# Half tiles of the experts' second product: finishing and summing two at a time, early in each of 16 rounds

## The chip, the cores and the metric

One Trainium2 chip, eight cores. Each core runs the same program on its own sequence (one of eight batch entries) and none waits for another. The metric is device microseconds (us) of the slowest core. TensorE (PE in the profile) does the matmuls, ScalarE (ACT) and VectorE (DVE) move results out of the 8 PSUM banks, GpSimd (POOL) and SyncE (SP) issue DMAs; POOL also does some arithmetic.

## The reference

Per sequence of 4096 rows of width 1024: one head of attention over the whole width with residual and layer norm, then a mixture of 64 experts chosen per group of 16 rows, with residual and layer norm again.

```python
x = _layernorm(x + _L0_attn_ref(x, W_qkv, b_qkv, W_out, b_out))
# _L0_ffn_ref, on groups of 16 rows:
sel   = jnp.einsum('...btd,...btes->...besd', grouped, perm)
inner = jax.nn.relu(jnp.einsum('...besd,desf->...besf', sel, f1) + bias)
inter = jnp.einsum('...besf,esfd->...besd', inner, f2)
out   = jnp.einsum('...besd,...btes->...btd', inter, perm)
x = _layernorm(x + out)
```

The change is in the last two einsums and the layer norm behind them.

## The kernel before

The program is written out by hand, one list of instructions for each engine, in the order in which Python code calls the helpers. An engine works through its list in that order; a wait in it (on a counter of another engine or of a DMA) holds up all that stands behind it. `T`, `VE`, `C`, `GP`, `SP` are the lists of TensorE, VectorE, ScalarE, GpSimd and SyncE. Nearly all matmuls carry line 128, ScalarE's operations line 137, VectorE's lines 142 to 149.

Attention comes first, the experts' first half (`gather`, `product1`, `rectify`) goes to about 1357 us, and the second half, with which this case deals, runs from there to the end. It is a loop of 16 **rounds**, `for j in range(16)`, each of eight **steps** k (lines 982 to 1006). In a round:

- `product2(j, k)`: 8 matmuls of 64x256 into a pair of banks. From round 3 on there are only two pairs for it, banks 0 to 3, used in turn (`made_in`). Step k issues the product of step k+1, the last step that of the next round's step 0. I call them p0 to p7.
- `product2_out(j, k, q)`: copies the pair (128x1024) to `arenaA`. From round 3 on, 0 to 6 are ScalarE's, 7 is VectorE's. I call them out0 to out7. Product p(k) needs out(k-2), which clears its pair.
- `swap(j - 1)`: one VectorE transpose of 128x4096 of the round before, into `xT`; it needs all eight outs of that round.
- `combine(m)`, from round 3, four in a round: one matmul of 128x512 with the identity, which brings the residual (`hrv(m)`, from `hsp`), and four of 32x512 (the experts' values from `xT` by the choices in `permC`) into one bank of 4 to 7. This is a **half tile**: 128 rows by 512 columns of the output. The bank must have been left by the half tile of the round before. Behind each `combine` SyncE loads the residual of the half tile four further on (`load_hr`). I call the four sums of a round c0 to c3.
- `stats2(m)`, at the end of the round: VectorE's `bn_stats` on each of the four banks; where the half tile is the second half of its rows (rounds 5, 6, 9, 10, 13, 14), an aggregate behind each.
- `finish2(m)`, from round 4, the four half tiles of the round before leave their banks, by ScalarE: f0 to f3. First halves (rounds 4, 5, 8, 9, 12, 13) are copied to `YF`. Second halves (rounds 6, 7, 10, 11, 14, 15, which I call **norm rounds**) are scaled and shifted on the way to one of five small homes, from which SyncE's queue stores them to `y`; ScalarE waits there for `home_used`, the last store out of that home. For output rows 0 to 1023 (rounds 6 and 7) the home is `i % 3`, so f0 and f3 of one round share one; later it goes round all five. POOL then scales the first half (line 844) and issues its store.
- in norm rounds ScalarE also computes four reciprocal deviations (`rstd2`, two tiny operations ahead of out0, which need VectorE's four aggregates of the round before), and VectorE the shifts (`shift2`, ahead of `swap`), for which f0 waits.

Before, the places in a round were: `swap` at step 2, f0 to f3 one at a step at steps 1 to 4, each behind that step's out, and c0 to c3 at steps 2 to 5, each behind that step's product. In round 15, step 2, POOL's list also takes the loads of the residuals 52, 53, 56 and 57, which need swap(14).

Behind the loop a tail sums and norms the last half tiles (`combine_last`, `keep_last`, `pair_last`, `second_last`, `first_last`); its first instructions need residuals that POOL loads behind all of its work on rounds 14 and 15. TensorE takes the residual 58 before it goes on.

Of the kernel before, what the change touches and what calls it, by code (L numbers as in the profile page):

```python
# [49 lines left out]
def build_nc():  # L50
# [47 lines left out]
    def bank(i):  # L98
        return PS[:, i * 512:(i + 1) * 512]
# [27 lines left out]
    def mm(out, lhsT, rhs, first, last, mark=False, **kw):  # L127
        fn = lambda e, o=out, l=lhsT, r=rhs, a=first, z=last, k=kw: e.matmul(o, l, r, start=a, stop=z, **k)  # L128
        if mark:
            return T.mark(fn)  # L130
        T.do(fn)
# [4 lines left out]
    def act(out, src, func, **kw):  # L136
        return C.mark(lambda e, o=out, s=src, f=func, k=kw: e.activation(o, s, f, **k))  # L137
# [556 lines left out]
    def place(m):  # L694

        s, i = m // 8, m % 8
        return s // 2, i, s % 2, s // 2 * 8 + i

    def summed_in(m):
        return m % 4 if 56 <= m < 60 else 4 + m % 4  # L700

    def hrv(m):
        if m >= 52:
            return A[:, INP[0] + (m - 52) * 512:INP[0] + (m - 51) * 512]
        return WC[:].bitcast(BF16)[:, (m % 4) * 512:(m % 4 + 1) * 512]

    def load_hr(m, q=SP):
        b, i, half, t = place(m)
        q.wait(c_tok[NT - 1], sw_tok[14] if m >= 52 else co_tok[m - 4] if m >= 4 else None)
        hr_ld[m] = dma(q, "hr%d" % (m % 4 if m < 52 else m - 48), hrv(m), hsp_d[t * 128:(t + 1) * 128, half * 512:(half + 1) * 512])  # L710

    def combine(m):
        b, i, half, t = place(m)
        bk = summed_in(m)
        T.wait(bank_free[bk], hr_ld[m], sw_tok[m // 8 * 2], sw_tok[m // 8 * 2 + 1])
        mm(bank(bk), IDT[:], hrv(m), True, False)
        vals = B[:, half * 16384:(half + 1) * 16384].rearrange("p (g d k w) -> p g d k w", g=16, k=2, w=2)
        for k in range(4):
            done = mm(bank(bk)[32 * k:32 * k + 32, :], PC[:, t * 128 + k * 32:t * 128 + (k + 1) * 32],
                      vals[:, 2 * i + k // 2, :, k % 2], False, True, mark=(k == 3), tile_position=(0, 32 * k))  # L720
        co_tok[m] = done
        if m + 4 < 52:
            load_hr(m + 4)
# [98 lines left out]
    def finish2(m):  # L822

        b, i, half, t = place(m)
        first = YF[:, i * 512:(i + 1) * 512]
        bk = summed_in(m)
        if not half:
            C.wait(st_tok[m], y_dma[m - 16] if m >= 16 else f1_tok[31, True])
            po_tok[m] = act(first, bank(bk), AF.Identity)
        else:  # L830
            o = MV + i * 2
            if b == 0:
                place_y = i % 3
            else:
                place_y = homes_taken[0] % 5
                homes_taken[0] += 1
            second = homes[place_y]
            C.wait(sh_tok[t // 4], home_used[place_y])
            C.wait(lgm_tok[NT - 1], s_tok[3, 7], s_tok[7, 7] if b else None)
            po_tok[m] = act(second, bank(bk), AF.Identity, scale=BN[:, RS + i:RS + i + 1], bias=BN[:, SH + i:SH + i + 1])  # L840
            SP.wait(po_tok[m])
            y_dma[m] = home_used[place_y] = dma(SP, "yb%d" % (place_y + 20), y_d[t * 128:(t + 1) * 128, 512:1024], second)
            GP.wait(sh_tok[t // 4], po_tok[m - 8])
            first_tok[m] = GP.mark(lambda e, f=first, o=o, i=i: e.tensor_scalar(  # L844
                f, f, BN[:, o:o + 1], BN[:, RS + i:RS + i + 1], ALU.subtract, ALU.mult))
            GP.wait(first_tok[m])
            y_dma[m - 8] = dma(GP, "ya%d" % i, y_d[t * 128:(t + 1) * 128, 0:512], first)
        bank_free[bk] = po_tok[m]
# [133 lines left out]
    for j in range(16):  # L982
        new, old = j >= 3, j >= 4
        norm = old and (j - 4) % 4 >= 2
        g = (j - 4) // 4 * 2 + (j - 4) % 2
        if norm:
            rstd2(g)
        for k in range(8):
            product2(*((j, k + 1) if k < 7 else (j + 1, 0)))
            if j < 3 or k < 7:  # L990
                    product2_out(j, k, VE if (j == 0 and k % 2 == 0) or (0 < j < 3 and k in (4, 6)) else C)
            if k == 0 and norm:
                shift2(g)
            if k == 2 and j > 0:
                swap(j - 1)
                if j == 15:
                    for m in (52, 53, 56, 57):
                        load_hr(m, GP)
            if new and 2 <= k <= 5:
                combine((j - 3) * 4 + k - 2)  # L1000
            if old and 1 <= k <= 4:
                finish2((j - 4) * 4 + k - 1)
        if new:
            for i in range(4):
                stats2((j - 3) * 4 + i)
            product2_out(j, 7, VE)
# [127 lines left out]
```

How the kernel before makes its waits and increments, by code:

```python
    def run(q, e):  # L1069
        for kind, a, b in q.ops:
            if kind == "wait":
                e.wait_ge(sems[a], b)
            elif kind == "do":
                a(e)
            elif kind == "mark":
                a(e).then_inc(sems[b], 1)
            else:
                a(e).then_inc(sems[b], 16)
```

## Time and profile before

| | |
|---|---|
| median of 3 runs | 1552.4 us (1550.98 to 1783.94) |
| the profiled execution | 1553.2 us |
| its span, slowest core (core 5) | 1551.6 us |
| spans of the 8 cores | 1545.1 to 1551.6 us |
| PE / DVE / ACT / POOL busy | 92% / 50% / 31% / 10% of the span |
| mean granted TensorE clock | 0.953 of full on core 5 |

A line of a timeline reads: start in us from the span's start, busy us, engine, line, operation, out<-in with shapes, number of instructions merged, and in brackets the idle time before it with what ended it. In the strips of the page the last five fortieths of the span (from 1357 us on) show the second half: VectorE and ScalarE are busy eight to nine tenths there, the granted clock is between 6 and 7 tenths, and TensorE falls from nine to seven tenths.

### The profile page before, as it was taken

What the parts mean: (1) busy time and instruction counts of PE and PEld (TensorE: products, weight loads), DVE (VectorE), ACT (ScalarE), POOL (GpSimd) and SP (SyncE); (2) the same over time, 40 slices, a digit from 0 to 9 for tenths busy, and PEclk for the clock granted to TensorE, in tenths of its full rate; (3) what the DMA queues carried; (4) which work ended last, traced back from release to release, by engine and by line L of the source; (5) the groups of instructions that cost most, each with busy time, mean ns of one, the idle gap of its engine ahead of it and who ended that gap; (6) DMA issues with size and microseconds to landing.
All of it is one profiled execution on the core that took longest, in us unless ns stands there. A gap on an engine that the chain in (4) does not pass through costs nothing.

```text
span 1551.6 us, 24544 instructions; the slowest of 8 cores (1545.1 to 1551.6 us)
## 1 busy us (share of the span) xinstructions
PE 1432.7 (92%) x8720; PEld 675.4 (44%) x8720; DVE 769.3 (50%) x1476; ACT 487.7 (31%) x825; POOL 159.6 (10%) x205
## 2 busy tenths in 40 slices
PE   5989999999999999999999999999999889967772
PEld 2434444444444444444444444444444467722220
DVE  2344424435434543552552454345355456698883
ACT  3330022122221222122212122212221267689883
POOL 0000000000000000000000000000010042005553
PEclk9999999999999999999999999999999899966765
DMA  9982005434744472543453456344134675304444
GB/s 282 297 260 97 1 16 89 81 63 89 115 83 76 82 119 52 101 82 75 89 109 75 79 100 108 68 85 86 29 88 80 160 247 162 124 28 156 154 155 150
DMA packets 222807, 170.30 MB, mean 110 GB/s; under 512 B 175296, under 2 KB 190288, under 8 KB 221664
## 3 DMA queue, kind: packets, MB, share of 16 engines
q1 hardware_dynamic: 214416, 132.75, 36.1%
q0 software_dynamic: 8128, 35.98, 10.5%
q8 instruction: 72, 1.18, 0.3%
q14 instruction: 47, 0.39, 0.1%
q10 hardware_dynamic: 144, 0.01, 0.0%
HBM read 118.62 MB, written 41.94 MB: 103 GB/s over the span
## 4 chain that ended last, share of the span: by engine, by line
PE 81%; DMA 6%; ACT 5%; issue 3%; DVE 2%; POOL 2%; SPq 0%; DVEq 0%; ACTq 0%; POOLq 0%
PE ps L128 81%; ACT arenaA L137 4%; DMA vw<-xt 2%; DMA vw<-wo 2%; DMA vw<-wkt 1%; DVE arenaA L142 1%; POOL arenaA L844 1%; DMA xT<-hsp 1%; DVE bnbuf L148 1%; DVE small L143 0%; POOL y L124 0%; SPq L124 0%; DMA arenaA<-hsp 0%; DMA arenaA<-arenaA 0%; DVE arenaA L144 0%
## 5 line engine op out<-in xcount | busy, mean ns | idle before, releaser
L128 PE MATMUL ps<-xT,arenaA 128*128 128x512 bf16 x2560 | 564.2, 379 | 7.9 <-ACT arenaA L137 7.9
L128 PE MATMUL ps<-vw,arenaA 128*128 128x512 bf16 (+1 forms) x3072 | 518.0, 369 | 38.3 <-ACT arenaA L137 17.4
L128 PEld LDWEIGHTS ps<-xT,arenaA 128*128 128x128 bf16 x2560 | 247.4, 98 | 301.3 <-issue 11.8
L128 PEld LDWEIGHTS ps<-vw,arenaA 128*128 128x128 bf16 (+1 forms) x3072 | 225.2, 106 | 319.1 <-issue 77.3
L137 ACT ACTIVATE arenaA<-ps,small 128x1024 bf16<-128x1024 f32 x128 | 141.4, 1110 | 519.1 <-DVE small L144 519.1
L146 DVE TENSOR_REDUCE small<-ps 128x1 f32<-128x512 f32 x256 | 175.7, 687 | 244.3 <-PE ps L128 244.1
L137 ACT ACTIVATE arenaA<-ps 128x512 bf16<-128x512 f32 (+2 forms) x303 | 209.1, 762 | 61.1 <-PE ps L128 59.0
L128 PE MATMUL ps<-arenaA,xT 128*128 128x128 bf16 (+1 forms) x1536 | 191.3, 276 | 12.7 <-ACT arenaA L137 8.0
L145 DVE SCALAR_TENSOR_TENSOR arenaA<-ps,small,arenaA 128x1024 f32<-128x1024 f32 x64 | 82.2, 1284 | 186.7 <-PE ps L134 139.0
L128 PEld LDWEIGHTS ps<-arenaA,xT 128*128 128x128 bf16 x1536 | 111.8, 99 | 91.8 <-issue 26.5
L142 DVE CAST arenaA<-ps 128x512 bf16<-128x512 f32 (+1 forms) x145 | 105.9, 762 | 45.8 <-PE ps L128 45.2
L124 POOL DMA_DIRECT2D hsp<-arenaA x32 | 18.3, 573 | 765.6 <-DVE arenaA L144 701.6
L137 ACT ACTIVATE arenaA<-ps,ubias 128x512 bf16<-128x512 f32 x64 | 44.0, 688 | 166.2 <-PE ps L128 166.2
L137 ACT ACTIVATE bnbuf<-bnbuf,small 128x1 f32<-128x1 f32 (+2 forms) x42 | 12.4, 295 | 215.4 <-DVE bnbuf L149 215.4
L143 DVE TENSOR_TENSOR small<-small 128x1 f32<-128x1 f32 (+1 forms) x192 | 35.4, 184 | 87.4 <-ACT small L137 70.4
L143 DVE TENSOR_TENSOR vw<-ps,permC 128x512 bf16<-128x512 f32 x64 | 44.1, 691 | 58.4 <-PE ps L128 58.4
L692 DVE STREAM_TRANSPOSE xT<-arenaA 128x4096 f32<-128x4096 f32 x16 | 71.1, 4444 | 1.4 <-DVE arenaA L142 0.5
L128 PE MATMUL ps<-arenaA 128*64 128x256 bf16 (+3 forms) x688 | 65.2, 294 | 6.2 <-ACT arenaA L137 3.0
L844 POOL TENSOR_SCALAR arenaA<-arenaA,bnbuf 128x512 f32<-128x512 f32 x24 | 49.7, 2072 | 135.4 <-DVE bnbuf L145 134.4
L148 DVE BATCH_NORM_STATS2 bnbuf<-ps 128x6 f32<-128x512 f32 x60 | 41.2, 688 | 23.7 <-PE ps L128 23.6
L128 PEld LDWEIGHTS ps<-arenaA 128*64 128x64 bf16 (+1 forms) x688 | 39.6, 112 | 27.5 <-issue 11.0
L128 PE MATMUL ps<-vw 128*128 128x512 bf16 x128 | 33.2, 421 | 16.5 <-DVE vw L142 12.8
(65 smaller groups left out, 606.8 us busy)
## 6 DMA issues: line engine op xcount, KB each, us to landing
vw<-xt SPq DMA_DIRECT2D x32, 512.0 KB, 9.5
arenaA<-x SPq DMA_DIRECT2D x32, 512.0 KB, 6.9
f1b<-f POOLq DMA_DIRECT2D x32, 256.0 KB, 5.8
hsp<-arenaA POOLq DMA_DIRECT2D x32, 256.0 KB, 3.8
f2b<-f POOLq DMA_DIRECT2D x32, 256.0 KB, 5.5
arenaA<-f1b SPq DMA_DIRECT2D x32, 256.0 KB, 3.7
vw<-f2b SPq DMA_DIRECT2D x8, 1024.0 KB, 6.1
y<-arenaA POOLq DMA_DIRECT2D x32, 256.0 KB, 3.2
```

The lines of the kernel that those rows point to most:

```text
L124: q.ops.append(("dma", lambda e, d=dst, s=src, k=kw: e.dma_start(d, s, **k), chan))
L128: fn = lambda e, o=out, l=lhsT, r=rhs, a=first, z=last, k=kw: e.matmul(o, l, r, start=a, stop=z, **k)
L137: return C.mark(lambda e, o=out, s=src, f=func, k=kw: e.activation(o, s, f, **k))
L142: copy = lambda e, *a, **k: e.tensor_copy(*a, **k)
L143: tt = lambda e, *a, **k: e.tensor_tensor(*a, **k)
L145: stt = lambda e, *a, **k: e.scalar_tensor_tensor(*a, **k)
L146: rmax = lambda e, *a, **k: e.reduce_max(*a, **k)
L148: bns = lambda e, *a, **k: e.bn_stats(*a, **k)
L692: sw_tok[j] = ve(lambda e, *a: e.transpose(*a), dst[:, (j % 2) * 128:(j % 2 + 1) * 128], src)
L844: first_tok[m] = GP.mark(lambda e, f=first, o=o, i=i: e.tensor_scalar(f, f, BN[:, o:o + 1], BN[:, RS + i:RS + i + 1], ALU.subtract, ALU.mult))
```

## The change

Three moves inside the loop of the 16 rounds; nothing is added or removed.

```diff
-            if k == 2 and j > 0:
+            if k == 0 and j > 0:
                 swap(j - 1)
                 if j == 15:
                     for m in (52, 53, 56, 57):
                         load_hr(m, GP)
-            if new and 2 <= k <= 5:
-                combine((j - 3) * 4 + k - 2)
-            if old and 1 <= k <= 4:
-                finish2((j - 4) * 4 + k - 1)
+
+            if old and k < 2:
+                finish2((j - 4) * 4 + 2 * k)
+                finish2((j - 4) * 4 + 2 * k + 1)
+            if new and 1 <= k <= 2:
+                combine((j - 3) * 4 + 2 * k - 2)
+                combine((j - 3) * 4 + 2 * k - 1)
```

f0 and f1 stand behind out0, f2 and f3 behind out1; c0 and c1 stand behind p2, c2 and c3 behind p3.

**ScalarE, the round after the first four finishes (round 5, a round without norm).** 128x128x8 is an out, 128x512 a finish. Before:

```order
L137 ACTIVATE arenaA<-ps 128x128x8 x4
L137 ACTIVATE arenaA<-ps 128x512
L137 ACTIVATE arenaA<-ps 128x128x8
L137 ACTIVATE arenaA<-ps 128x512
L137 ACTIVATE arenaA<-ps 128x128x8
L137 ACTIVATE arenaA<-ps 128x512
L137 ACTIVATE arenaA<-ps 128x128x8
L137 ACTIVATE arenaA<-ps 128x512
L137 ACTIVATE arenaA<-ps 128x128x8 x2
```

Now:

```order
L137 ACTIVATE arenaA<-ps 128x128x8 x6
L137 ACTIVATE arenaA<-ps 128x512 x2
L137 ACTIVATE arenaA<-ps 128x128x8
L137 ACTIVATE arenaA<-ps 128x512 x2
L137 ACTIVATE arenaA<-ps 128x128x8 x5
```

The four outs ahead of the first finish were out5 and out6 of the round before with out0 and out1; now six outs stand together (out2 to out6 with out0 of the next round), and only out1 stands between the two pairs of finishes.

**TensorE, from c0 of round 3 to c0 of round 4.** 64x256 x8 is one product; wcrow,identb with the four xT,permC behind it is one sum. Before:

```order
L128 MATMUL ps<-vw,arenaA 64x256 x224
L128 MATMUL ps<-wcrow,identb 128x512
L128 MATMUL ps<-xT,permC 32x512 x4
L128 MATMUL ps<-vw,arenaA 64x256 x8
L128 MATMUL ps<-wcrow,identb 128x512
L128 MATMUL ps<-xT,permC 32x512 x4
L128 MATMUL ps<-vw,arenaA 64x256 x8
L128 MATMUL ps<-wcrow,identb 128x512
L128 MATMUL ps<-xT,permC 32x512 x4
L128 MATMUL ps<-vw,arenaA 64x256 x8
L128 MATMUL ps<-wcrow,identb 128x512
L128 MATMUL ps<-xT,permC 32x512 x4
```

Now:

```order
L128 MATMUL ps<-vw,arenaA 64x256 x216
L128 MATMUL ps<-wcrow,identb 128x512
L128 MATMUL ps<-xT,permC 32x512 x4
L128 MATMUL ps<-wcrow,identb 128x512
L128 MATMUL ps<-xT,permC 32x512 x4
L128 MATMUL ps<-vw,arenaA 64x256 x8
L128 MATMUL ps<-wcrow,identb 128x512
L128 MATMUL ps<-xT,permC 32x512 x4
L128 MATMUL ps<-wcrow,identb 128x512
L128 MATMUL ps<-xT,permC 32x512 x4
L128 MATMUL ps<-vw,arenaA 64x256 x56
```

A product stood between any two sums, and five products (x40) between rounds. Now one product, p3, stands between two pairs of sums, and seven (p4 of this round to p2 of the next) follow without a sum.

**POOL, in round 15.** The four loads 52, 53, 56 and 57 against the scaling operations (L844) and their stores:

```order
 L844 TENSOR_SCALAR arenaA<-arenaA,bnbuf 128x512
 L124 DMA y<-arenaA 128x512
+L124 DMA arenaA<-hsp 128x512 x4
 L844 TENSOR_SCALAR arenaA<-arenaA,bnbuf 128x512
 L124 DMA y<-arenaA 128x512
-L124 DMA arenaA<-hsp 128x512 x4
 L844 TENSOR_SCALAR arenaA<-arenaA,bnbuf 128x512
```

The loads moved ahead of one scaling and its store. VectorE's list is unchanged row by row. SyncE's has the same loads and stores, in runs of four instead of in turn.

## Rows read from the trace of the kernel before

**Rows 1.** The head of the page.

```profile
span 1551.6 us, 24544 instructions; the slowest of 8 cores (1545.1 to 1551.6 us)
```

**Rows 2.** Busy time by stretches, rounds 4 to 15: their sum.

```profile
sum 124.00, PE 93.23 PEld 27.57 DVE 105.03 ACT 110.93 POOL 59.87; mean PE 7.77 PEld 2.30 DVE 8.75 ACT 9.24 POOL 4.99
```

**Rows 3.** Timeline of ScalarE: out0 of rounds 3, 9 and 15, and round 9.

```profile
1376.84 3.86 ACT L137 ACTIVATE arenaA<-ps 128x1024 bf16<-128x1024 f32 x4 [0.90 <-PE ps L128]
...
1437.32 1.02 ACT L137 ACTIVATE arenaA<-ps 128x1024 bf16<-128x1024 f32 x1 [0.72 <-PE ps L128]
1438.79 6.65 ACT L137 ACTIVATE arenaA<-ps 128x1024 bf16<-128x1024 f32 x9 [0.45 <-PE ps L128]
1445.68 1.02 ACT L137 ACTIVATE arenaA<-ps 128x1024 bf16<-128x1024 f32 x1 [0.24 <-PE ps L128]
1447.74 0.30 ACT L137 ACTIVATE bnbuf<-bnbuf,small 128x4 f32<-128x4 f32 x1 [1.04 <-DVE bnbuf L149]
...
1499.78 1.01 ACT L137 ACTIVATE arenaA<-ps 128x1024 bf16<-128x1024 f32 x1
```

**Rows 4.** Timeline of VectorE in round 9: swap, second statistics, last aggregate, out7.

```profile
1438.17 4.45 DVE L692 STREAM_TRANSPOSE xT<-arenaA 128x4096 f32<-128x4096 f32 x1
...
1443.63 0.70 DVE L148 BATCH_NORM_STATS2 bnbuf<-ps 128x6 f32<-128x512 f32 x1
1444.50 0.21 DVE L149 BATCH_NORM_AGGREGATE bnbuf<-bnbuf 128x2 f32<-128x12 f32 x1 [0.17 <-DVE bnbuf L148]
...
1447.35 1.20 DVE L142 CAST arenaA<-ps 128x1024 bf16<-128x1024 f32 x1
```

**Rows 5.** Timeline of TensorE in round 9: p1 and p2, c0, p4, c3, p0.

```profile
1438.21 0.91 PE L128 MATMUL ps<-vw,arenaA 64*64 64x256 bf16 x16 [1.06 <-DVE arenaA L142]
...
1440.72 0.58 PE L128 MATMUL ps<-wcrow,identb 128*128 128x512 bf16 x1
...
1441.78 0.64 PE L128 MATMUL ps<-vw,arenaA 64*64 64x256 bf16 x8
1442.35 0.61 PE L128 MATMUL ps<-wcrow,identb 128*128 128x512 bf16 x1
...
1445.50 0.39 PE L128 MATMUL ps<-wcrow,identb 128*128 128x512 bf16 x1
...
1446.16 0.41 PE L128 MATMUL ps<-vw,arenaA 64*64 64x256 bf16 x8
...
1446.85 0.41 PE L128 MATMUL ps<-vw,arenaA 64*64 64x256 bf16 x8 [0.28 <-ACT arenaA L137]
```

**Rows 6.** Stretches of 1 us: from:to, length, PE busy, clock, DMA share, GB/s.

```profile
1438.00:1439.00 1.00, 0.79 (x16) 0.71 0.00 0
...
1443.00:1444.00 1.00, 1.00 (x12) 0.50 0.43 119
...
1446.00:1447.00 1.00, 0.72 (x20) 1.00 0.48 131
```

**Rows 7.** Timeline of ScalarE in round 6: f0, the out behind it, f3.

```profile
1408.68 0.77 ACT L137 ACTIVATE arenaA<-ps,bnbuf 128x512 f32<-128x512 f32 x1
1409.34 1.02 ACT L137 ACTIVATE arenaA<-ps 128x1024 bf16<-128x1024 f32 x1
...
1413.78 0.78 ACT L137 ACTIVATE arenaA<-ps,bnbuf 128x512 f32<-128x512 f32 x1 [0.25 <-DMA y<-arenaA]
```

**Rows 8.** Timeline of VectorE in round 15: swap(14).

```profile
1500.31 4.43 DVE L692 STREAM_TRANSPOSE xT<-arenaA 128x4096 f32<-128x4096 f32 x1
```

**Rows 9.** Timeline of POOL: first and fifth scaling from round 14 on, the loads.

```profile
1489.79 2.06 POOL L844 TENSOR_SCALAR arenaA<-arenaA,bnbuf 128x512 f32<-128x512 f32 x1 [14.76 <-DVE bnbuf L145]
...
1502.88 2.07 POOL L844 TENSOR_SCALAR arenaA<-arenaA,bnbuf 128x512 f32<-128x512 f32 x1
...
1506.10 2.13 POOL L124 DMA_DIRECT2D arenaA<-hsp  x4
...
1518.23 2.13 POOL L124 DMA_DIRECT2D arenaA<-hsp  x4
```

## The prediction

> **What bounds the kernel now.** The page's head gives the span of 1551.6 us [rows 1]; the profiled time is 1553.2, 1.6 more, and 0.8 above the median of 1552.4. The change touches only the last fifth, so I went from the strips of the page to a table by stretches, one stretch to a round. Over rounds 4 to 15 (124 us) ScalarE is busy 110.9 us, VectorE 105.0, TensorE 93.2 [rows 2]. The reader should see that none is full: the round is a loop through all three engines, and the question is which waits remain on ScalarE, which is nearest to full.
>
> The timeline of ScalarE answers that. From out0 of round 3 to out0 of round 15 it is 1499.78 - 1376.84 = 122.94 us for 12 rounds, 10.25 us each [rows 3]. In round 9 ScalarE stands idle 0.72 us ahead of out0, 0.45 ahead of out1, 0.24 ahead of out6, and 1.04 ahead of the next round's reciprocal deviations. The first is p0 of the next round, which can't start until out6 has cleared its pair: it is there before and after. The second is p1, which waits for out7 on VectorE. The third is TensorE itself. The fourth is the last aggregate on VectorE.
>
> The timeline of VectorE shows why that aggregate is late: swap takes 4.45 us, a statistic and its aggregate take 0.87 to the aggregate's start and about 0.97 from pair to pair, so swap plus four pairs is 4.37 + 3.9 = 8.3 us, but from the start of swap to the start of out7 it is 9.2 [rows 4]. The 0.9 between is waiting for sums.
>
> TensorE: a product takes 0.57 us from start to start and a sum 1.06, while the last sum of the round takes 0.66 [rows 5]. The granted clock tells them apart: 0.50 in a stretch in which TensorE never stopped, 1.00 three us later [rows 6], that is 1.2 and 2.4 GHz. A product is then 0.57 or about 0.34 (I take it in the sum's ratio of 0.66 to 1.06). In the steps with a sum TensorE needs 1.63 us at the lower clock, ScalarE 1.4 to 1.6: TensorE sets the pace in the middle of the round.
>
> **The change, part by part.** I put t = 0 at the start of out0 and lay one round of the new order out with the durations above. An out starts 0.95 after the one before it ((3.86 - 1.02)/3) and is done after 1.02; the four unscaled finishes add 6.65 - 1.02 - 4 x 0.95 = 1.83, 0.46 each [rows 3]; scaled ones add 0.66 each [rows 7]. From a done out to the product behind it is 0.15 us (out6 done at 1446.70, p0 at 1446.85 [rows 5]), and since ScalarE waits 0.72 for a p0 of 0.41, from a done product to its out it is 0.16.
>
> *What is taken away.* Out1 has two finishes ahead of it, so p1 has 0.9 to 1.3 us more: the wait of 0.45 goes. The sums are ready when swap ends, so the statistics follow it: the 0.9 goes, and most of the 1.04. With these two alone a round would be bounded by ScalarE: 7 outs and 4 finishes with a wait of 0.72 is 8.55 + 0.72 = 9.3 us without norm and 9.36 + 0.72 = 10.1 with it. Of the 12 rounds 7 are without and 5 with norm: 65.1 + 50.5 = 115.6 us, 7.3 less than now.
>
> *What it costs on TensorE.* Its list is in order, so p3 stands behind c0 and c1, and p4 behind c2 and c3. p2 starts at 1.02 + 0.15 = 1.17. At the lower clock: p2 to 1.74, c0 to 2.80, c1 to 3.86, p3 to 4.43, c2 to 5.49, c3 to 6.55, p4 to 7.12, so out4 can start at 7.28. ScalarE, back to back, would want it at 4 x 0.95 + 1.83 = 5.6, in norm rounds at 3.8 + 2.64 = 6.4. At the full clock TensorE waits for ScalarE instead and nothing is lost. So the clock decides: bound from above 7.28, from below 5.6 (6.4). The rows are a mix: the first sums of a round ran at 1.06, the last at 0.66. I take that mix, c3 and p4 fast: c3 to 6.15, p4 to 6.49, out4 at 6.65. Then out4, out5, out6 take 2 x 0.95 + 1.02: done at 9.6. The wait for p0 is 0.72, or 0.95 if it runs at the lower clock (0.64 instead of 0.41 in the rows): 0.85. A round is 10.45 us, with norm or without, since the reciprocal deviations fit into that wait. Twelve of them are 125.4: **+2.5 us**. (All slow: 9.6 + 0.63, wait 0.95, 11.2 a round, +11. All fast: -7.3.)
>
> The Trainium skill speaks for the fast case. "TensorE: Matmul & The Clock Gate", the section on HAM oscillation, advises to put matmuls together so that the engine stays at full clock; by it, packing the sums would raise the clock in them and the sum would take the -7.3. The rows lean against it here, as TensorE was already busy without a gap in a stretch at 0.50 [rows 6], and by them the sum is +2.5.
>
> *What it costs at the homes.* In round 6 f0 starts at 1408.68 and f3, with the same home, is released by f0's store at 1413.78: 5.10 us [rows 7]. Before, that cost 0.25. Now f3 could start 0.66 + 0.66 + 0.95 + 0.66 = 2.9 us behind f0, and waits the rest, 2.2. Behind it stand c3 and out2. With f0 at 0.95, f3 runs from 6.05 to 6.8, c3 from 6.95 to 8.0, p4 to 8.6, out4 at 8.75, out6 done at 11.7, the round 12.5 long: 2.0 more than 10.45. Round 7 shares homes alike. If the store lands sooner by what four stores in turn take from each other, less; it can't be below nothing. I take **+3.9** for both, bounds 0 and +4.4. From round 10 on a home comes back after five finishes, a round later, and costs nothing.
>
> *What it costs on POOL.* POOL is the chain at the end: eight scalings and stores of rounds 14 and 15, 3.28 us each, four loads of 2.13 together, and then the load of residual 58 at 1518.23 [rows 9], for which TensorE waits. Before, POOL had no gap: the four loads, which need swap(14), stood behind the fifth scaling. Now they stand behind the fourth store, which is over at 1502.88, and swap(14) ends at 1504.74 [rows 8]; POOL stands still 1.86 us and everything behind it moves, residual 58 too. This holds as long as round 14 keeps about its length, since swap(14) comes a round behind the first scaling: **+1.8**, bounds +1.2 and +2.5 for a round shorter or longer by 0.6 to 0.7.
>
> *At no cost.* SyncE's loads of residuals are in runs of four, but each is for a sum a round (10 us) later. First halves have to wait for POOL's stores of the round before last; POOL is through with them in its pause (14.76 us ahead of round 14, [rows 9]). VectorE's list is the same; if its cover went, it would be bounded by 8.3 + 1.3 = 9.6 us a round, below 10.45.
>
> **The sum.** 1552.4 + 2.5 + 3.9 + 1.8 = 1560.6; I say 1561.
>
> **The rivals.**
> - *The clock comes up in the packed sums.* Then TensorE hides behind ScalarE: -7.3 + 4.3 (homes: 2.17 each, not hidden) + 1.2 = -1.8: 1551. For it: TensorE is then busy in one piece from 1.2 on. Against it: the seven products behind stand alone, 0.4 busy in 0.95, and in round 9 the clock was falling (0.71) in such a stretch, behind p7, p0 and a wait for out7 [rows 6].
> - *Faster: the same with the homes' stores landing in time.* The chain is VectorE's: statistics and out7 no longer wait. -7.3 + 1.2 = -6: 1546. It decides if f0's store lands within 2.9 us of f0's start; 5.1 were seen, so this is the weakest.
> - *The clock stays at 1.2 GHz through p4 in every round.* +11 + 2.6 (12.5 - 11.2, twice) + 2.5 = +16: 1568.5.
> - *The gain is hidden anyway*: waits only move from one place in the round to another, and the round stays at 10.25: 0 + 3.9 + 1.8: 1558. This can't be told from the forecast by its time, only by the trace.
>
> **How the numbers follow.** The forecast and the last rival together, 1556 to 1565: 0.50. All slow, 1565 to 1570: 0.17. Full clock, 1549 to 1556: 0.19. Faster, below 1549: 0.09. Over 1570 by something I haven't seen: 0.05. The range takes in the first three: 1549.5 to 1569.5. The bound of 2% (31 us, about what a measurement of this kernel can tell from no change) is far outside of all of them: faster 0.01, the same 0.96, slower 0.03.
>
> **What would show it.** Right: ScalarE idle ahead of out4 for 0.2 to 1.1 us in every round, ended by TensorE; no wait ahead of out1; statistics directly behind swap; f3 in rounds 6 and 7 idle about 2 us, ended by a DMA to y; POOL idle some 2 us ahead of its four loads in round 15. Wrong: clock at 1.00 by c2 and no wait ahead of out4 (first rival); f3 without a wait; or the load of 58 still 28.4 us behind POOL's first scaling of round 14, as in rows 9.

## The result and the profile after

The changed kernel takes 1560.4 us (median of 7 runs), the kernel before 1553.9 in the same job: ratio 1.0046, interval 1.0036 to 1.0056, so 7 us slower. The forecast was 1561, worked out as +8.6 on a base of 1552.4. The profiled execution has a span of 1558.8 us on its slowest core, core 1, against 1551.6 [rows 1]. (A few executions of every kernel here, up to 1798 us, fall into a slower state of the chip that has nothing to do with the kernel; the ratios leave them out.)

ScalarE's timeline, core 1: round 3, rounds 4, 5 and 6, and out0 of round 15. It answers [rows 3, 7].

```profile
1377.20 2.94 ACT L137 ACTIVATE arenaA<-ps 128x1024 bf16<-128x1024 f32 x3 [0.90 <-PE ps L128]
1381.86 1.02 ACT L137 ACTIVATE arenaA<-ps 128x1024 bf16<-128x1024 f32 x1 [1.72 <-PE ps L128]
1384.54 2.85 ACT L137 ACTIVATE arenaA<-ps 128x1024 bf16<-128x1024 f32 x3 [1.65 <-PE ps L128]
1388.29 5.73 ACT L137 ACTIVATE arenaA<-ps 128x1024 bf16<-128x1024 f32 x8 [0.90 <-PE ps L128]
1395.28 2.85 ACT L137 ACTIVATE arenaA<-ps 128x1024 bf16<-128x1024 f32 x3 [1.25 <-PE ps L128]
1399.08 5.73 ACT L137 ACTIVATE arenaA<-ps 128x1024 bf16<-128x1024 f32 x8 [0.94 <-PE ps L128]
...
1410.51 1.44 ACT L137 ACTIVATE arenaA<-ps,bnbuf 128x512 f32<-128x512 f32 x2
...
1413.73 0.78 ACT L137 ACTIVATE arenaA<-ps,bnbuf 128x512 f32<-128x512 f32 x1 [0.19 <-DMA y<-arenaA]
1414.40 4.81 ACT L137 ACTIVATE arenaA<-ps 128x1024 bf16<-128x1024 f32 x5
...
1505.21 1.02 ACT L137 ACTIVATE arenaA<-ps 128x1024 bf16<-128x1024 f32 x1 [0.41 <-PE ps L128]
```

A round now has eight operations in one piece (out0 to out3 and the four finishes, 5.73 us), then a wait for TensorE, then out4 to out6 (2.85), then the wait for p0. The wait ahead of out1 is gone, the wait ahead of out4 is new: 1.25 us in round 4, and in round 3, which has no finishes, 1.72 ahead of out3 and 1.65 ahead of out4. From out0 of round 3 to out0 of round 15 it is 128.0 us, against 122.9.

TensorE in round 9 of the same core: c0, c1, p3, c2 and c3, p4 with p5, and p6; then VectorE in that round. They answer [rows 5] and [rows 4].

```profile
1442.15 0.53 PE L128 MATMUL ps<-wcrow,identb 128*128 128x512 bf16 x1 [0.18 <-issue]
...
1443.16 0.61 PE L128 MATMUL ps<-wcrow,identb 128*128 128x512 bf16 x1
...
1444.25 0.64 PE L128 MATMUL ps<-vw,arenaA 64*64 64x256 bf16 x8
1444.82 0.61 PE L128 MATMUL ps<-wcrow,identb 128*128 128x512 bf16 x1
...
1445.82 0.39 PE L128 MATMUL ps<-wcrow,identb 128*128 128x512 bf16 x1
...
1446.48 0.63 PE L128 MATMUL ps<-vw,arenaA 64*64 64x256 bf16 x16
1448.17 0.41 PE L128 MATMUL ps<-vw,arenaA 64*64 64x256 bf16 x8 [1.06 <-ACT arenaA L137]
```

```profile
1440.76 4.45 DVE L692 STREAM_TRANSPOSE xT<-arenaA 128x4096 f32<-128x4096 f32 x1
1445.13 0.66 DVE L148 BATCH_NORM_STATS2 bnbuf<-ps 128x6 f32<-128x512 f32 x1
1445.96 0.21 DVE L149 BATCH_NORM_AGGREGATE bnbuf<-bnbuf 128x2 f32<-128x12 f32 x1 [0.17 <-DVE bnbuf L148]
...
1449.84 1.23 DVE L142 CAST arenaA<-ps 128x1024 bf16<-128x1024 f32 x1 [0.76 <-PE ps L128]
```

Three sums at the lower clock (1.09 from c1 to p3), the fourth in 0.66, then p4 and p5 back to back, and out4 at 1447.00. The statistics follow swap without a wait, but out7, which before waited for nobody [rows 4], now waits 0.76 us for p7. The aggregates are early, and nobody needs them that early.

The waits of ScalarE, summed: first the changed kernel, core 1, from 1377 to 1505 us, then the kernel before, core 5, from 1377 to 1500 us.

```profile
ACT arenaA L137 <- PE ps L128: 19.9, 23, 1.7
ACT arenaA L137 <- DMA y<-arenaA: 0.4, 2, 0.2
```

```profile
ACT arenaA L137 <- PE ps L128: 10.1, 20, 0.9
ACT bnbuf L137 <- DVE bnbuf L149: 4.7, 6, 1.0
```

So the change does what it is built for, it takes away the 4.7 us of waiting for VectorE's aggregates; TensorE takes back 9.8.

POOL from round 14 on, core 1, answers [rows 9]:

```profile
1494.94 2.07 POOL L844 TENSOR_SCALAR arenaA<-arenaA,bnbuf 128x512 f32<-128x512 f32 x1 [17.39 <-DVE bnbuf L145]
...
1507.38 0.60 POOL L124 DMA_DIRECT2D y<-arenaA  x1 [0.56 <-POOL arenaA L844]
1510.56 2.13 POOL L124 DMA_DIRECT2D arenaA<-hsp  x4 [2.58 <-DVE xT L692]
...
1525.95 2.13 POOL L124 DMA_DIRECT2D arenaA<-hsp  x4
```

POOL stands still 2.58 us for swap(14), which ends at 1510.00; the loads begin 0.56 us behind that. From POOL's first scaling to the load of residual 58 it is 31.0 us, against 28.4.

The eight cores run the same program, but not with the same clock. Cores 2, 3 and 5 of the changed kernel, two with a high clock and between them one with a low one, 1380 to 1490 us (columns: length, busy us of PE, PEld, DVE, ACT and POOL, granted clock, DMA share, GB/s):

```profile
1380.00:1490.00 110.00, 71.38 (x879) 24.07 (x890) 89.95 (x87) 97.16 (x129) 45.35 (x34) 0.79 0.39 131
...
1380.00:1490.00 110.00, 82.28 (x883) 25.14 (x879) 87.69 (x85) 91.72 (x120) 42.68 (x32) 0.69 0.39 128
...
1380.00:1490.00 110.00, 77.88 (x907) 24.30 (x900) 92.20 (x92) 97.97 (x129) 48.15 (x37) 0.80 0.42 138
```

Cores 2 and 5 had 0.79 and 0.80 and took 113.8 and 112.9 us from swap(2) to swap(13); the six others had 0.69 to 0.75 and took 115.2 to 117.2. The eight spans go from 1546.8 to 1558.8, before from 1545.1 to 1551.6.

### The profile page after: what moved, and what is told of

Same layout as the page of the kernel before. It is cut to its first block, busy times and chain, and to the rows that moved or that the text cites. A ratio compares the mean times of both kernels' runs of the same rounds, so it can differ in the third digit from the quotient of the medians.

```text
span 1558.8 us, 24543 instructions; the slowest of 8 cores (1546.8 to 1558.8 us)
## 1 busy us (share of the span) xinstructions
PE 1429.4 (92%) x8720; PEld 675.9 (43%) x8720; DVE 767.4 (49%) x1476; ACT 487.6 (31%) x825; POOL 159.5 (10%) x205
## 3 DMA queue, kind: packets, MB, share of 16 engines
q0 software_dynamic: 8128, 35.98, 10.4%
## 4 chain that ended last, share of the span: by engine, by line
PE 83%; ACT 5%; DMA 5%; issue 3%; DVE 2%; POOL 1%; SPq 1%; ACTq 0%; DVEq 0%; POOLq 0%
PE ps L128 83%; ACT arenaA L137 5%; DMA vw<-xt 2%; DMA vw<-wqt 1%; DMA vw<-wkt 1%; DMA xT<-hsp 1%; SPq L124 1%; DVE arenaA L142 1%; POOL arenaA L844 0%; DVE bnbuf L148 0%; DVE small L143 0%; DMA arenaA<-arenaA 0%; POOL y L124 0%; DMA arenaA<-hsp 0%; DVE arenaA L144 0%
## 5 line engine op out<-in xcount | busy, mean ns | idle before, releaser
L844 POOL TENSOR_SCALAR arenaA<-arenaA,bnbuf 128x512 f32<-128x512 f32 x24 | 49.8, 2073 | 140.2 <-DVE bnbuf L145 139.1
L128 PE MATMUL ps<-vw 128*128 128x512 bf16 x128 | 31.6, 406 | 19.2 <-DVE vw L142 14.7
L148 DVE BATCH_NORM_STATS2 bnbuf<-ps 128x6 f32<-128x512 f32 x60 | 39.2, 674 | 10.8 <-PE ps L128 10.8
## 6 DMA issues: line engine op xcount, KB each, us to landing
vw<-xt SPq DMA_DIRECT2D x32, 512.0 KB, 10.7
```

The source lines that it names most:

```text
L148: bns = lambda e, *a, **k: e.bn_stats(*a, **k)
```

## The experiments

In the table, the rounds are the time from the start of swap(2) to the start of swap(13) in VectorE's timeline, the clock is the granted clock in that stretch, and the waits are the idle time of ScalarE in its timeline from swap(3) to swap(13), ended by TensorE / by VectorE; each is the median of the eight cores of the profiled execution. "Tail" is POOL's time from its first scaling of round 14 to its second batch of residual loads. Ratios are against the kernel before, timed in the same job on the same chip. There were four jobs: the change by itself; loads_back to pairs_only; single_early to filler; and the last four. Times of different jobs can be compared only through their ratios.

| kernel | ratio (95%) | rounds, us | clock | waits PE / DVE | tail |
|---|---|---|---|---|---|
| before | 1 | 111.4 | 0.74 | 6.8 / 4.2 | 28.4 |
| the change | 1.0046 (1.0036 to 1.0056) | 116.2 | 0.70 | 15.1 / 0 | 30.7 |
| loads_back | 1.0039 (1.0025 to 1.0053) | 116.0 | 0.72 | 14.5 / 0 | 28.4 |
| loads_only | 1.0025 (1.0013 to 1.0037) | 112.4 | 0.73 | 6.8 / 4.7 | 30.9 |
| finish_only | 1.0098 (1.0083 to 1.0113) | 125.6 | 0.66 | 16.7 / 6.8 | 29.6 |
| pairs_only | 1.0083 (1.0068 to 1.0098) | 124.0 | 0.56 | 22.4 / 0 | 28.7 |
| single_early | 1.0060 (1.0039 to 1.0082) | 120.4 | 0.615 | 17.1 / 0.7 | 28.4 |
| pairs_late | 1.0054 (1.0036 to 1.0072) | 119.1 | 0.745 | 15.9 / 1.0 | 28.4 |
| single_late | 1.0187 (1.0166 to 1.0209) | 137.9 | 0.665 | 19.2 / 13.9 | 30.9 |
| filler | 1.0049 (1.0031 to 1.0067) | 114.9 | 0.805 | 12.0 / 0 | 30.5 |
| filler_full | 0.9990 (0.9962 to 1.0017) | 113.5 | 0.82 | 10.8 / 0 | 28.5 |
| step_finish | 0.9995 (0.9977 to 1.0013) | 111.0 | 0.765 | 6.2 / 5.4 | 28.4 |
| step_early | 0.9972 (0.9943 to 1.0001) | 106.5 | 0.775 | 5.3 / 1.2 | 28.4 |
| step_fill | 0.9970 (0.9952 to 0.9989) | 107.0 | 0.79 | 5.7 / 1.4 | 28.4 |

In the code of the runs the steps of the finishes and sums stand as tables, `{step: (which, ...)}`; where a run keeps the places of the kernel that it is compared with, the table says the same as that kernel's lines.

### POOL's loads

**loads_back.** The changed kernel with the loads behind the first scaling of round 15:

```diff
-                if j == 15:
-                    for m in (52, 53, 56, 57):
-                        load_hr(m, GP)
...
             if old:
                 for i in {0: (0, 1), 1: (2, 3)}.get(k, ()):
                     finish2((j - 4) * 4 + i)
+                    if j == 15 and i == 0:
+                        for m in (52, 53, 56, 57):
+                            load_hr(m, GP)
```

> The changed kernel, but with POOL's four residual loads of round 15 behind the first scaling and its store, as before the change. Theory: the loads' new place costs POOL its standstill of 2.1 to 3 us ahead of them (28.4 us from the first scaling of round 14 to the load of residual 58 before, 30.4 to 31.5 after, by core). So the stretch should be 28.4 again and the time 2.6 us below the changed kernel: +4.5 us against the kernel before, ratio 1.003. Rival: the tail's start is set by something else (TensorE's or ScalarE's end of round 15), then the time stays at +7, ratio 1.0046.

The tail is 28.45 us again, 2.3 less than the median of the changed kernel. The ratio fell from 1.0046 to 1.0039, 1 us; the intervals leave room for 4 less and for 2 more. The ratio alone can't say whether the tail's term counts in full. The traces can: from the start of swap(13) to the end of its span a core takes 61.3 to 62.1 us here, as before the change (61.0 to 62.2), and 63.4 to 64.7 in the changed kernel. That is 2.4 us in the median, the term at its full size.

**loads_only.** The kernel before with those loads where the change has them:

```diff
-            if k == 2 and j > 0:
+            if k == 0 and j > 0:
                 swap(j - 1)
                 if j == 15:
                     for m in (52, 53, 56, 57):
                         load_hr(m, GP)
```

> The kernel before, with nothing but POOL's four residual loads of round 15 moved ahead of the first scaling of that round. Theory: POOL stands still until swap(14) is done, 1.9 us in the rows of before; +2 us, ratio 1.0013; rounds 3 to 13 as before (111.4 us from swap(2) to swap(13), median of the cores). Rival (hidden): 0.

Ratio 1.0025, 3.9 us, with an interval of 2 to 5.7: slower beyond doubt, though nothing else was changed, and twice what I expected. The tail grew by 2.5, the stretch from swap(13) to the end by 2.4 (64.4 against 61.9, medians). The rounds grew by 1.0 in the median, which the change in round 15 can't have caused; I take that for the scatter of a single profile. By their ratios the two runs put the loads between 1 and 4 us. The 2.4 of the traces lies between them.

POOL stands still 2.47 or 2.48 us on all eight cores, not the 1.9 of the expectation, although round 14 has its old length (10.5 us from the first scaling to swap(14)). The difference is the 0.57 us from the end of swap to the first load.

### The two halves of the change

**finish_only.** Finishes as in the change, sums one at a time behind p3 to p6 as before, loads as before:

```diff
-            if old and 1 <= k <= 4:
-                finish2((j - 4) * 4 + k - 1)
+            if old:
+                for i in {0: (0, 1), 1: (2, 3)}.get(k, ()):
+                    finish2((j - 4) * 4 + i)
```

> Only the finishes moved (f0, f1 behind out0, f2, f3 behind out1); the sums one at a time behind p3 to p6 as before, POOL's loads as before. Theory: p3 now waits for out1, which has two finishes ahead of it (t about 3.0 instead of 2.6, in norm rounds 3.4), and TensorE sets the pace from there on: +0.3 to +0.5 a round, +3 to +6 us, ratio 1.002 to 1.004; the wait ahead of out1 goes. Rival: the finishes early are the good half of the change (out1's wait of 0.2 to 0.45 goes each round and TensorE has no pairs in its way): -3 to -5 us.

1.0098: 15 us slower, twice the change as a whole and more than twice what I expected. The direction was the theory's (out1, and p3 behind it, come later), the size was not: the clock is down to 0.66, and VectorE's aggregates are late again (6.8 us), since the sums, which follow p3, start later with it. I had left out that the clock may change with the order. The tail is 29.6 us, although the loads stand where they did: with the longer rounds swap(14) comes so late that POOL waits for it there too (1.20 us on core 1; in single_late, below, 1.58 on core 0).

**pairs_only.** Finishes as before, sums in pairs behind p3 and p5:

```diff
-            if new and 2 <= k <= 5:
-                combine((j - 3) * 4 + k - 2)
+            if new:
+                for i in {2: (0, 1), 4: (2, 3)}.get(k, ()):
+                    combine((j - 3) * 4 + i)
```

> Only the sums in pairs: finishes one at a time at steps 1 to 4 as before, c0 and c1 behind p3, c2 and c3 behind p5, POOL's loads as before, so the mean place of the sums is the one of before. Theory: a product behind two sums at 1.2 GHz (2.1 us) comes later than ScalarE wants it, whatever the place in the round: +0.3 to +0.5 us a round, +3 to +6 us in all, ratio 1.002 to 1.004, with idle time of ScalarE ahead of the out behind each pair. Rival: pairing itself is harmless and only being early costs: 0.

1.0083, again above the expected 1.002 to 1.004. In this place pairing is not harmless. The second sum of each pair waits for its finish, as TensorE's timeline shows (core 5, round 8: c0, c1, p4, c2, c3 and the next products):

```profile
1435.05 0.58 PE L128 MATMUL ps<-wcrow,identb 128*128 128x512 bf16 x1
...
1436.45 0.58 PE L128 MATMUL ps<-wcrow,identb 128*128 128x512 bf16 x1 [0.27 <-ACT arenaA L137]
...
1440.03 0.59 PE L128 MATMUL ps<-wcrow,identb 128*128 128x512 bf16 x1 [0.36 <-ACT arenaA L137]
...
1441.09 1.07 PE L128 MATMUL ps<-vw,arenaA 64*64 64x256 bf16 x16
1443.01 1.28 PE L128 MATMUL ps<-vw,arenaA 64*64 64x256 bf16 x16 [0.85 <-ACT arenaA L137]
```

TensorE is never idle for more than 0.85 us here, but nothing in this round runs at the higher clock: sums 1.06 to 1.09, products 0.64, the granted clock 0.50 from 1433 to 1444. ScalarE waits 22.4 us for TensorE in all. How much of the 13 us is the pairs and how much the clock, this run can't tell.

### Where the sums stand

**single_early, pairs_late, single_late.** Finishes in early pairs as in the change, loads as before; only the steps of the sums differ (against loads_back):

```diff
-                for i in {1: (0, 1), 2: (2, 3)}.get(k, ()):
+                for i in {1: (0,), 2: (1,), 3: (2,), 4: (3,)}.get(k, ()):
                     combine((j - 3) * 4 + i)
```

(pairs_late: `{2: (0, 1), 4: (2, 3)}`; single_late: `{3: (0,), 4: (1,), 5: (2,), 6: (3,)}`.)

> Finishes in early pairs as in the change, but the sums one at a time, each behind p2, p3, p4, p5; POOL's loads as before. Theory: TensorE needs 1.63 us a step at the lower clock and starts a step earlier than before, so out4 finds its product (t 5.2 against 5.6) and out5, out6 wait 0.4 at most: a round of about 10.1, that is -2 us against before, ratio 0.9987 (and 7 below the changed kernel less the 2.6 of the loads). No wait of 1 us ahead of out4. Rival: early sums cost as such, by the early low-clock stretch: +3 to +5.

> Finishes in early pairs as in the change, the sums in pairs behind p3 and p5 (as in the run with pairs only); POOL's loads as before. Theory: two sums at 1.2 GHz still come between a product and the next, so ScalarE waits after each pair; about +4 to +7 us, ratio 1.003 to 1.0045. Rival: with both finishes early the pairs don't wait themselves and ScalarE has outs in store: 0 to +2.

> Finishes in early pairs, the sums one at a time and late, behind p4, p5, p6, p7; POOL's loads as before. Theory: the early products p2 to p4 are never in the way, but the last sum delays p0 of the next round and the statistics and with them out7 and the aggregates: +2 to +5 us against before, the waits ahead of out0 and of the deviations longer than 1 us. Rival: place does not matter as long as the sums are single: within 1 us of the run with single early sums.

single_early is a miss: 1.0060 where I expected 0.9987. TensorE, core 0, in round 9: p2, p3, p4, p5 and c3. The idle time ahead of a product is in brackets; c0 to c2 stand between.

```profile
1447.06 0.64 PE L128 MATMUL ps<-vw,arenaA 64*64 64x256 bf16 x8 [0.69 <-ACT arenaA L137]
...
1448.95 0.64 PE L128 MATMUL ps<-vw,arenaA 64*64 64x256 bf16 x8 [0.17 <-ACT arenaA L137]
...
1450.85 0.64 PE L128 MATMUL ps<-vw,arenaA 64*64 64x256 bf16 x8 [0.16 <-ACT arenaA L137]
...
1452.51 0.64 PE L128 MATMUL ps<-vw,arenaA 64*64 64x256 bf16 x8
1453.08 0.61 PE L128 MATMUL ps<-wcrow,identb 128*128 128x512 bf16 x1
```

p3 and p4 wait for out1 and out2, since two finishes stand together ahead of each of these. And nothing in the round ran at the higher clock, not even the last sum, which took 0.66 before the change and after it. What kept the clock down the run can't tell; waits of this size alone don't, as step_early below shows. A round is 11.0 us (out0 at 1434.88 and 1445.89). pairs_late is somewhat above its range (1.0054, expected 1.003 to 1.0045; its interval reaches down to 1.0036), with the clock of before (0.745): its waits for TensorE, 15.9 against 6.8 us, don't need a lower clock. single_late is far beyond its range (1.0187): VectorE can't finish its statistics before out7, and ScalarE waits 13.9 us for the aggregates on top.

### The clock

**filler.** The changed kernel with half of p5, p6 and p7 done once more ahead of themselves:

```diff
-        for m in range(2):
+        for m, a, z in ([(0, True, True)] if j >= 3 and k in (5, 6, 7) else []) + [(0, True, False), (1, False, True)]:
...
-                              m == 0, m == 1, mark=(m == 1 and h == 1 and r == 1))
+                              a, z, mark=(m == 1 and h == 1 and r == 1))
```

> The changed kernel, with half of the products p5, p6 and p7 done once more ahead of themselves (12 matmuls of 64x256 instead of 8, the first four a repeat whose result is overwritten), from round 3 on: work for TensorE in the stretch in which it has none, hidden while the out before runs (0.51 + 0.31 us at full clock against 0.95). Theory: what the packed sums cost is the clock of 1.2 GHz in which they run; if TensorE is kept busy its clock stays up through them (1.00 in the sums, 0.66 each), the wait ahead of out4 goes and the time falls 4 to 9 us below the changed kernel: -2 to +3 against before. Rival: the clock falls all the same or the wait ahead of out4 does not depend on it: +7 to +10.

**filler_full.** All of p5, p6 and p7 done twice, on the base of loads_back:

```diff
-        for m in range(2):
+        for m, last in ([(0, False), (1, False)] if j >= 3 and k in (5, 6, 7) else []) + [(0, True), (1, True)]:
...
-                              m == 0, m == 1, mark=(m == 1 and h == 1 and r == 1))
+                              m == 0, m == 1, mark=(last and m == 1 and h == 1 and r == 1))
```

> Twice the work in p5, p6 and p7 (16 matmuls instead of 8), sums and finishes as in the changed kernel, POOL's loads as before: to be compared with the changed kernel with its loads put back (116.0 us from swap(2) to swap(13), clock 0.72, ScalarE waits 14.5 us for TensorE in rounds 3 to 13), and with half the filler (114.9, 0.805, 12.0). Theory: the clock comes up further (0.85 and more), the wait ahead of out4 falls further, below 12 us in all though each filled product now costs ScalarE 0.1; rounds 113 to 115. Rival (the list order alone holds out4 up, whatever the clock): 116 or more, clock up or not.

More work for TensorE makes the kernel faster. filler_full is 0.9990 against loads_back's 1.0039, with intervals that do not touch. The two ratios lie 7.5 us apart, but they come from two jobs on two chips. In the profiled executions the rounds take 113.5 against 116.0 us, and from swap(13) on both take the same (61.8 and 61.6): 2.5 us is what the traces show. The waits for TensorE are 10.8 against 14.5, the clock 0.82 against 0.72, a little under the 0.85 that I expected.

The half filler is a miss in its time. It raised the clock (0.805) and shortened the rounds to 114.9, but the ratio is 1.0049 (with the loads in it), in the range of its rival. In its trace f3 waits up to 2.52 us for its home in rounds 6 and 7, on six cores over 0.5, which in the changed kernel happens on none: here is the wait that I had forecast there.

Not every round gained. ScalarE and TensorE, core 0 of filler_full: rounds 12 and 13, then c0 of round 12 to p5.

```profile
1471.47 8.55 ACT L137 ACTIVATE arenaA<-ps 128x1024 bf16<-128x1024 f32 x11 [0.72 <-PE ps L128]
1480.74 5.73 ACT L137 ACTIVATE arenaA<-ps 128x1024 bf16<-128x1024 f32 x8 [0.72 <-PE ps L128]
1487.36 2.93 ACT L137 ACTIVATE arenaA<-ps 128x1024 bf16<-128x1024 f32 x3 [0.89 <-PE ps L128]
```

```profile
1473.40 0.38 PE L128 MATMUL ps<-wcrow,identb 128*128 128x512 bf16 x1 [0.35 <-issue]
...
1474.70 0.41 PE L128 MATMUL ps<-vw,arenaA 64*64 64x256 bf16 x8
1475.13 0.38 PE L128 MATMUL ps<-wcrow,identb 128*128 128x512 bf16 x1
...
1476.43 0.41 PE L128 MATMUL ps<-vw,arenaA 64*64 64x256 bf16 x8
1477.34 0.63 PE L128 MATMUL ps<-vw,arenaA 64*64 64x256 bf16 x16 [0.50 <-ACT arenaA L137]
```

In round 12 all four sums run at the higher clock, two of them in 1.30 us where the lower clock takes 2.1. p4 is there in time, nothing waits ahead of out4, and the round takes 9.27 us, ScalarE's bound. In round 13 the sums are slow again, and out4 waits 0.89. The same holds in the traces of the changed kernel, loads_back and filler_full, which have one order. The table takes their rounds 4, 5, 8, 9, 12 and 13, which have no norm, where the trace has all four sums. A sum counts as slow if its first matmul takes over 0.56 us, as fast if it takes under 0.45; a round is the time from swap to swap.

| sums at the lower clock | rounds seen | wait ahead of out4, us | round, us |
|---|---|---|---|
| all four | 20 | 1.24 to 1.72 | 10.7 to 11.2 |
| the first three | 47 | 0.81 to 1.06 | 10.1 to 10.8 |
| the first two | 13 | 0.36 to 0.63 | 9.7 to 10.0 |
| none | 11 | none | 9.3 to 9.5 |

(17 more rounds, with a first or last sum between the two or a fast first one, have waits of 0.87 to 0.89 and take 10.2 to 10.4 us.) The rounds with none are all of filler_full. So with the order unchanged the wait ahead of out4 goes with the clock of the sums, and at the full clock it is gone whole. What decides whether a round gets that clock is not shown: core 7 of filler_full has four slow sums in round 8 and none in round 12, with the same work.

### One step earlier, singly

**step_finish, step_early, step_fill.** Not pairs, but each finish and each sum one step earlier than before; loads as before:

```diff
-            if new and 2 <= k <= 5:
-                combine((j - 3) * 4 + k - 2)
-            if old and 1 <= k <= 4:
-                finish2((j - 4) * 4 + k - 1)
+            if old:
+                for i in {0: (0,), 1: (1,), 2: (2,), 3: (3,)}.get(k, ()):
+                    finish2((j - 4) * 4 + i)
...
+            if new:
+                for i in {1: (0,), 2: (1,), 3: (2,), 4: (3,)}.get(k, ()):
+                    combine((j - 3) * 4 + i)
```

(step_finish moves the finishes alone; step_fill adds half a filler to p6 and p7.)

> Only the finishes one step earlier, singly (behind out0 to out3); sums where they were, POOL's loads as before. Theory: ScalarE's wait ahead of out1 (0.2 to 0.45 us) is filled with f0, but the sums set TensorE's pace from p3 on as before and VectorE's aggregates stay late: within 1 us of before a round-sum of 111.4, ratio 0.999 to 1.001. Rival (any early finish costs, as with the pairs at 1.0098): above 1.004.

> The kernel before with each finish and each sum one step earlier, still one at a time: f0 to f3 behind out0 to out3, c0 to c3 behind p2 to p5; POOL's loads as before. So far every arrangement in which TensorE's middle stretch (products and sums) had a gap or a wait in it lost the clock there (mean granted clock from swap(2) to swap(13) 0.56 to 0.66, before 0.74) and was 0.6 to 2% slower. Theory: here p2 to c3 follow without a gap (f0 lies in the wait that ScalarE has ahead of out1), the clock is that of before (0.74), the statistics are ready when swap ends, and ScalarE's waits for VectorE (4.2 us before, 0 after) go without the waits for TensorE growing by 8: rounds 2 to 13 take 107 to 110 us instead of 111.4, ratio 0.997. Rival (early sums cost as such): 114 to 120 us, ratio 1.002 to 1.006.

> As the run with all one step earlier, and half of the products p6 and p7 done once more ahead of themselves (12 matmuls instead of 8, result overwritten) from round 3 on. Theory: if the clock in the sums is what is left, it comes up (0.80) and the rounds take another 1 to 3 us less than without it. Rival: ScalarE and VectorE already bound the round, the clock comes up and the time stays.

The times of step_finish and step_early are as the theory has them. step_finish is level (0.9995), the rounds 111.0. step_early has rounds of 106.5, 4.9 less than before and a little below the forecast 107, and is 0.9972; its interval just touches 1, that of step_fill (0.9970) does not, and in both the rounds of all eight cores are shorter than those of any core before. ScalarE, core 7 of step_early, rounds 8, 9 and the start of 10, then TensorE in round 9, c0, p3 and c1:

```profile
1426.72 8.48 ACT L137 ACTIVATE arenaA<-ps 128x1024 bf16<-128x1024 f32 x11 [0.72 <-PE ps L128]
1435.92 8.48 ACT L137 ACTIVATE arenaA<-ps 128x1024 bf16<-128x1024 f32 x11 [0.72 <-PE ps L128]
1444.92 0.30 ACT L137 ACTIVATE bnbuf<-bnbuf,small 128x4 f32<-128x4 f32 x1 [0.52 <-DVE bnbuf L149]
```

```profile
1437.68 0.38 PE L128 MATMUL ps<-wcrow,identb 128*128 128x512 bf16 x1 [0.18 <-ACT arenaA L137]
...
1438.49 0.41 PE L128 MATMUL ps<-vw,arenaA 64*64 64x256 bf16 x8
1439.09 0.38 PE L128 MATMUL ps<-wcrow,identb 128*128 128x512 bf16 x1 [0.18 <-ACT arenaA L137]
```

All eleven operations of a round stand in one piece, with one wait of 0.72 us: 9.2 us a round, what I had reckoned (9.3) as ScalarE's bound. step_early beats the changed kernel by its ratio, and the kernel before by its rounds.

The reason that I had given, that a gap or a wait in TensorE's middle stretch costs the clock, is not borne out. pairs_late, with 0.745, had already spoken against it. In step_early itself the sums don't follow without a gap: in this round each waits 0.18 us for its finish, and yet all run at the higher clock. ScalarE still waits 1.2 us for VectorE, not 0. The filler adds nothing (rounds 107.0, clock 0.79): its theory, another 1 to 3 us less, missed, and its rival came. Singly placed, slow sums cost less: round 8 had two of them and took the same 9.2 us. The eight rounds without norm with three or four slow sums took 9.8 to 10.0, all others at most 9.7.

## Why the prediction was right, and where it was not

The time (1561 against 1560.4) was right, and so was the mechanism of its first term, products late behind two sums. The homes, the largest term, were wrong. Two terms of the sum were off in opposite directions, and their agreement is partly luck: rounds forecast at +6.4 (2.5 and 3.9) measured +5.1 on core 1, +4.8 in the median of the cores; POOL's +1.8 measured +2.4. A further 1.5 us is the base, 1552.4 in the forecast and 1553.9 in the job of the result: +8.6 was forecast, and +6.5 measured by the medians, +7 by the ratio.

**The waits taken away: right.** The wait ahead of out1 is gone, ScalarE's wait for aggregates went from 4.7 to 0 us, the statistics follow swap directly. ScalarE's bound of 9.3 us a round was reached by step_early.

**Products behind two sums: right in kind, too small.** I forecast out4 waiting 0.2 to 1.1 us in every round and +2.5 in all. Measured on core 1: 1.65, 1.25, 1.03, 0, 0, 0.88, 0.88, 0.28, 1.15, 1.67, 1.31 and 0.49 in rounds 3 to 14, and the twelve rounds took 5.1 us more, nearly nothing of which is homes. The step that failed is the mix of clocks, three sums slow and the fourth fast with p4, which I took from one round and put in all of them. On the eight cores of the changed kernel it held in 44 of the 69 rounds whose four sums the trace has; in 21 all four were slow, among them rounds 3, 4, 11, 12 and 13 of core 1. What such a round costs stands in the table of the fillers. Round 3, which I had taken to be like the others, lost 1.8 us by itself, as it has no finishes between out1 and out3 and waits for p3 as well. The average round is 10.67 us instead of 10.45. In rounds 6 and 7 of core 1 there was no wait, as the scaled finishes took the time.

**The homes: wrong.** I took +3.9 us, measured about nothing: f3 of round 6 began 3.2 us behind f0 and waited 0.19. The step that failed is the landing time of f0's store, read from one row [rows 7] as 5.1 us from f0's start as though it were fixed. In the kernel before SyncE issued that store at 1409.5 and residual loads and POOL's store were in flight with it; in the changed kernel SyncE issued it at 1411.35 and it had landed by 1413.73, 2.4 us later, with POOL's first store issued only at 1412.74. The stated lower bound of nothing was the case, and "f3 without a wait" was one of the signs of being wrong that I had named. (The term was also added up loosely: twice the 2.0 of its own working is 4.0 or 4.1, not 3.9.) That it is the company of the other transfers that made it late was not tested; filler, with waits up to 2.5 us at the same place, shows that the landing time varies between kernels.

**POOL's loads: right, somewhat small.** +1.8 forecast, bounds 1.2 and 2.5; the stretch grew by 2.0 to 3.1 us on the eight cores. What was left out is the time from the end of swap(14) to the first load, 0.56 or 0.57 us on every core: the sum let the loads begin the moment swap ends. The length of round 14 gives the rest (10.0 to 11.1 us from the first scaling to swap(14), against 10.5). By the ratios the loads are worth 1 (loads_back) to 4 us (loads_only), by the stretch from swap(13) to the end 2.4.

**The rivals.** The full clock through the sums did not come in the changed kernel: packing the sums did not raise it. Cores 2 and 5, with 0.79 and 0.80, went some of the way (3 us less than the others). In filler_full it came in 11 rounds without norm, and they took the 9.3 to 9.5 us that this rival gives a round. The homes' stores landed in time, as the second rival wanted, but without the higher clock its 1546 could not come. All slow did not come in every round, but in 21 of 69. That the waits would only move and the round stay at 10.25 is refuted by the rounds, 10.67.

**What the forecast did not see** was the reverse side of its own argument. It treated the clock as given. finish_only was expected to lose 0.2 to 0.4% and lost 1%, single_early to gain 0.1% and lost 0.6%, and with it went clocks of 0.66 and 0.615. single_early and step_early differ in nothing but the finishes (in pairs, or one behind each out), and are 13.9 us apart in the rounds. Part of that is order: with one finish ahead of it p3 comes 0.5 to 0.7 us sooner (an estimate, the length of one finish). Part is the clock, 0.615 against 0.775. Their rounds without norm, sorted as above, tell the parts roughly: with four slow sums 10.5 to 11.0 us in single_early and 10.0 in step_early; with none slow 9.3 (two rounds only), and 9.3 to 9.5. So the order of the finishes costs 0.5 to 1 us a round at the lower clock, and at the higher one nothing that shows. But single_early has four slow sums in 23 of 36 such rounds, step_early in 4 of 36. Why the order of ScalarE's finishes should do that to TensorE's clock stays open.

## What to carry to other kernels

Where one engine runs two kinds of work in order, of which one feeds a double-buffered loop, put one piece of the other kind between each two of the first, not two pieces at once. In pairs_only the total work and its mean place were those of before, and the kernel was 0.8% slower. At TensorE's higher clock the pairs of the change cost nothing, at the lower one up to 1.7 us of waiting a round. Look where each moved instruction delays the next link of the loop (here f1 ahead of out1, c1 ahead of p3), and not only whose wait it shortens. And don't take TensorE's clock as given when its order changes: read the granted clock of the stretch in each variant beside its waits.

## What the runs showed of the hardware

The granted clock is not a property of a kernel only: in one execution, eight cores with the same program stood at 0.69 to 0.80 over 110 us, and the two with the highest clock were 1.4 to 4.3 us ahead over eleven rounds. The order of ScalarE's finishes alone went with a change of TensorE's clock from 0.775 to 0.615. Doubling the matmuls of three products in each round, 24 more of 64x256, went with a clock of 0.82 against 0.72 and made eleven rounds 2.5 us shorter (filler_full against loads_back, medians of the cores). Core 7 of filler_full ran all four sums of round 12 at 2.4 GHz and all four of round 8 at 1.2 GHz, with the same work. Gaps of 0.18 us ahead of every sum did not keep the clock down in round 9 of step_early. From the end of a VectorE transpose to the load on POOL that waited for it, it was 0.56 or 0.57 us. And 256 KB stores of round 6 of the changed kernel landed anywhere between 2.3 and 4.8 us after their issue (core 1).
